# Order of the first loads, the gate block of the last stage, and the products of the linear attention

## The chip, the cores and the metric

The kernel runs on one core of a Trainium2 chip. The metric is the device time of one execution in microseconds; lower is better. TensorE does matrix products into PSUM (eight banks of 512 four-byte columns per partition), VectorE, ScalarE and GpSimd work on rows, SyncE issues most DMAs. Each engine runs its own instructions in the order in which they are written; semaphores tie the engines together.

## What is computed

A decoder of twelve layers (stages 0 to 11), each followed by a layer norm of the sum with its input, on 8 sequences of 100 tokens of 256 features, with a context of 361 tokens per sequence. All arithmetic is in four-byte floats. Two layers matter here. Stage 6 is a gated linear attention with 8 heads of 32 features:

```
q, k, v = (heads(Wq), heads(Wk), heads(Wv))     # of the rms-normed x; q, k rotated (rope)
beta, ig, og = (gate(Wbeta, bbeta), gate(Wig, big), gate(Wog, bog))
def step(M, inp):                               # over the tokens
    q_t, k_t, v_t, f_t, g_t, o_t = inp          # f = beta, g = ig, o = og
    M = M * f_t[..., None, None] + g_t[..., None, None] * scale * (k_t[..., :, None] * v_t[..., None, :])
    y_t = jnp.einsum('bhd,bhde->bhe', q_t, M) * o_t[..., None]
```

The kernel writes the recurrence out as a decayed mask per head (a scan over the tokens), which multiplies the scores of q and k before they multiply v. Stage 11 is a mixture of experts, of which this is the head and the end:

```
def _rmsnorm(x, g):
    return x * jax.lax.rsqrt(jnp.mean(x * x, axis=-1, keepdims=True) + eps) * g
scores = jax.nn.sigmoid(u @ centroids)
gpk, i_topk = jax.lax.top_k(scores, K)          # K = 2 of 8
gk = gpk / scores.sum(axis=-1, keepdims=True)
return u + h_s + h_r                            # and x + this, so x twice
```

## The kernel before

Everything is written by hand in blocks: a block holds one list of instructions per engine, and at its exit all engines meet. The order inside a list is the order of the code; no scheduler changes it. X holds the tokens (100 partitions, 8 batches, 256), XT their transpose (features on partitions), ps the eight PSUM banks. `program` runs the stages one after another; ahead of each stage SyncE issues the load of the next stage's weights (its "pack"), and the four computing engines wait for the stage's own pack.

**Start** (L3766 to L3774, in `program`). SyncE issues five loads: features (XT), pack 0, tables, tokens (X), context (ctxT). It waits for features, tables and tokens (a count of 48), then the block ends and stage 0 begins with projections of XT. The context has a semaphore of its own, waited for at stage 1. The tables hold the identity for transposes and the masks.

**Stage 6, `l2_attn`.** A hardware loop of two turns, each with four batches (TURN = 4, index j). In a turn TensorE transposes the normed tokens into hT; computes per batch v with the gates (L3120, one bank, 280 columns) and then q and k (L3125, the next bank, four parts of 128 features by 100 tokens); then the rotated q and k of all batches (L3133, with weights whose halves are swapped); then beta turned (L3139) and spread over the rows (L3144), the scores (L3151), the heads (L3157), the turned output (L3162) and the output product (L3167). VectorE copies v out of PSUM, makes the rotation in three instructions per batch (sine product L3204, cosine product L3206, sum L3208), scans the decayed mask (L3213, two per batch), weighs it with the scores (L3220, two per batch), and does the norm. ScalarE copies q and k and makes the gates' sigmoid. GpSimd makes the entries of the scan (L3099) and, after each rotation, a padded q (L3103): q repeated for the four heads that share a tile of 128 features, with the other heads' rows zeroed, so that a score product runs over all 128 rows.

**Stage 11, `l3_ffn`.** First block: logits on TensorE (L2479), sigmoid on ScalarE, the choice of two of eight and the gates on VectorE, the gates turned on TensorE (L2499) and stored by ScalarE (L2504); SyncE loads the first expert's weights. Second block: VectorE squares and sums the tokens (L2940), GpSimd makes the root per batch (L2915, L2917), VectorE scales (L2944) and doubles X (L2946) in turn, TensorE transposes each batch into its own bank (L2924), ScalarE copies it twice with two gains (L2933 into xs, L2934 into xr). Then `experts` runs 40 experts' units, and `experts_tail` the last norm.

## Time and profile before

| | us |
|---|---|
| median of 3 runs | 2661.86 |
| lowest, highest | 2661.77, 2664.53 |
| profiled execution, whole time | 2663.2 |
| profiled execution, span | 2661.4 |
| TensorE busy in the span | 2260.9 (85%) |
| VectorE busy | 1539.0 (58%) |
| ScalarE busy | 1147.5 (43%) |
| GpSimd busy | 466.6 (18%) |
| mean granted TensorE clock | 0.902 of 2.4 GHz |

The busy times are sums over stages with different limits. Stage 6 takes from about 1329 to 1450 us of the span, the head of stage 11 from 2263 to 2287. The profile's timeline gives each instruction's start and duration, and in square brackets how long its engine had stood idle and what ended that; "PEld" is TensorE's weight load.

### The profile page before, as it was taken

The numbers are of one execution on the slowest core, as the hardware profiler recorded it, in microseconds if no ns is written. First come the engines' busy times: TensorE is split into PE (matmuls) and PEld (weight loads), VectorE is DVE, ScalarE is ACT, GpSimd is POOL, SyncE is SP. The second block draws the span as 40 slices with busy tenths as digits, with TensorE's granted clock in tenths as the row PEclk, the third lists the DMA queues.
The fourth block names the chain that finished last, engine by engine and source line by source line (L and its number), as shares of the span: only waits on it lengthen the run. The fifth ranks groups of instructions, "written<-read, shape, count | busy, mean of one in ns | idle before, by whom it ended". The sixth has DMA issues, their size and how long they took to land. (4 is left out here: it accounts for less than half of the span.)

```text
span 2661.4 us, 42960 instructions
## 1 busy us (share of the span) xinstructions
PE 2260.9 (85%) x15050; PEld 1791.9 (67%) x15050; DVE 1539.0 (58%) x3604; ACT 1147.5 (43%) x3103; POOL 466.6 (18%) x681
## 2 busy tenths in 40 slices
PE   6799664659999976879878969799987999899997
PEld 4566432227777744569867648799975665799997
DVE  3566658996555653545555535456544555555555
ACT  4566344543434424533211634343321565455553
POOL 0200018982000010100143410000013222100001
PEclk8899788899999986669988979899977999799999
DMA  3000012210000013324200024232200000233331
GB/s 108 9 2 2 32 66 76 71 53 32 1 1 1 1 49 117 97 103 149 78 36 5 1 60 125 75 110 90 90 33 9 6 8 1 86 107 109 104 110 61
DMA packets 46180, 151.37 MB, mean 57 GB/s; under 512 B 16967, under 2 KB 19115, under 8 KB 43960
## 3 DMA queue, kind: packets, MB, share of 16 engines
q1 hardware_dynamic: 46012, 149.21, 17.6%
q8 instruction: 96, 1.57, 0.2%
q14 instruction: 72, 0.59, 0.1%
HBM read 137.70 MB, written 11.50 MB: 56 GB/s over the span
## 5 line engine op out<-in xcount | busy, mean ns | idle before, releaser
L2410 PE MATMUL ps<-l1a_zc,tables_sb 128*128 128x400 f32 x256 | 107.8, 553 | 96.3 <-POOL l1a_zc L2339 60.3
L2410 PEld LDWEIGHTS ps<-l1a_zc,tables_sb 128*128 128x128 f32 x256 | 46.9, 200 | 157.1 <-POOL l1a_zc L2339 88.5
L1912 ACT ACTIVATE l1x_probs<-ps,l1x_nmax 100x361 f32<-100x361 f32 x128 | 70.7, 558 | 164.5 <-DVE l1x_nmax L1987 164.5
L2350 POOL TENSOR_TENSOR l1a_dbx<-l1a_dx,l1a_rows 128x400 f32<-128x400 f32 x128 | 130.3, 1055 | 7.0 <-DMA l1a_rows<-l1a_rows_spilled 4.9
L2758 DVE TENSOR_TENSOR l3f_act_out<-l3f_act_out,l3f_gates 128x800 f32<-128x800 f32 x80 | 79.4, 993 | 81.8 <-ACT l3f_act_out L2714 81.8
L2762 DVE TENSOR_TENSOR l3f_hg_low<-l3f_act_out,l3f_hg_high 128x800 fp32r<-128x800 f32 x80 | 79.5, 993 | 62.9 <-ACT l3f_hg_high L2720 62.9
L2714 ACT ACTIVATE l3f_act_out<-ps,l3f_biases 128x800 f32<-128x800 f32 x80 | 74.3, 929 | 91.7 <-PE ps L2603 90.7
L2363 ACT ACTIVATE ps<-l1a_delta,weights 128x400 f32<-128x400 f32 x128 | 76.5, 598 | 81.2 <-DVE ps L2393 53.2
L2602 PE MATMUL ps<-l3f_x_high,l3f_w_high 128*128 128x400 f32 x320 | 111.4, 348 | 0.0
L2601 PE MATMUL ps<-l3f_x_high,l3f_w_low 128*128 128x400 f32 x320 | 110.7, 346 | 0.5 <-DVE l3f_w_low L2692 0.5
L2603 PE MATMUL ps<-l3f_x_low,l3f_w_high 128*128 128x400 f32 x320 | 110.6, 346 | 0.0
L2602 PE MATMUL ps<-l3f_hg_high,l3f_w_high 128*128 128x400 f32 x320 | 110.2, 344 | 0.0
L2601 PE MATMUL ps<-l3f_hg_high,l3f_w_low 128*128 128x400 f32 x320 | 110.0, 344 | 0.0
L2603 PE MATMUL ps<-l3f_hg_low,l3f_w_high 128*128 128x400 f32 x320 | 110.0, 344 | 0.0
L1026 ACT ACTIVATE l3x_probs<-l3x_s_sb,l3x_nmax 100x361 f32<-100x361 f32 x128 | 75.3, 589 | 68.3 <-DVE l3x_nmax L1115 64.3
L2720 ACT ACTIVATE l3f_hg_high<-l3f_act_out 128x800 fp32r<-128x800 f32 x80 | 69.9, 874 | 72.4 <-PE ps L2603 62.5
L1024 ACT ACTIVATE l0x_probs<-ps,l0x_nmax 100x361 f32<-100x361 f32 x128 | 70.7, 557 | 64.8 <-DVE l0x_nmax L1122 57.9
L2602 PE MATMUL ps<-l2f_x_high,l2f_w_high 128*128 128x400 f32 x272 | 95.0, 349 | 0.0
L2601 PE MATMUL ps<-l2f_x_high,l2f_w_low 128*128 128x400 f32 x272 | 94.3, 347 | 0.0
L2603 PE MATMUL ps<-l2f_x_low,l2f_w_high 128*128 128x400 f32 x272 | 94.2, 346 | 0.0
L2393 DVE TENSOR_TENSOR_SCAN ps<-ps,l1a_dbx 128x400 f32<-128x400 f32 x86 | 84.6, 994 | 16.7 <-POOL l1a_dbx L2350 9.8
L1115 DVE CUSTOM_DVE_ANT_0 l3x_s_sb<-ps,l3x_mask_b 100x361 f32<-100x361 f32 x128 | 63.2, 531 | 44.7 <-PE ps L931 44.4
(662 smaller groups left out, 6454.7 us busy)
## 6 DMA issues: line engine op xcount, KB each, us to landing
l3f_landing<-l_ffn_units SPq DMA_DIRECT2D x40, 513.0 KB, 3.6
l3f_gates<-l3f_gates SPq DMA_DIRECT2D x40, 400.0 KB, 3.4
l2x_a_taps<-l2x_taps_spread SPq DMA_DIRECT2D x8, 1912.5 KB
l2f_landing<-l_ffn_units SPq DMA_DIRECT2D x17, 771.0 KB, 4.5
l1a_rows<-l1a_rows_spilled SPq DMA_DIRECT2D x32, 400.0 KB, 3.4
l1f_gates<-l1f_gates SPq DMA_DIRECT2D x16, 800.0 KB, 4.1
l1f_positions<-l1f_staged SPq DMA_DIRECT2D x16, 621.9 KB
l1f_landing<-l_ffn_units SPq DMA_DIRECT2D x16, 512.0 KB, 3.2
```

The costliest lines, as they stand in the source:

```text
L1024: last = act.activation(probs[:, n % 2, r, 0:KEYS], score_bank(r), ACT.Exp, bias=nmax[:, n % 2, r:r + 1], accum_out=sums)
L1026: last = act.activation(probs[:, n % 2, r, 0:KEYS], s_sb[:, h % 3, r % 2, :], ACT.Exp, scale=-1.0, bias=nmax[:, n % 2, r:r + 1], accum_out ...
L2350: pool.tensor_tensor(dbx[:, n % BUFS, :], dx[:, j, m, :], rows[:, g % RING, 0, :], ALU.mult).then_inc(s.dbx_ready, 1)
L2363: act.activation(da(n), delta_h[:, m, j, :], ACT.Exp, scale=a_log[:, m, i:i + 1]).then_inc(s.da_ready, 1)
L2393: dve.tensor_tensor_scan(z(n), da(n), dbx[:, n % BUFS, :], 0.0, ALU.mult, ALU.add).then_inc(s.scan_done, 1)
L2410: pe.matmul(y_bank(m), st.ident, zc[:, n % DONE, :], start=(i == 0), stop=(i == NS - 1)).then_inc(s.sum_done, 1)
L2601: pe.matmul(out, r(w_lo), r(x_hi), start=start, stop=False)
L2602: pe.matmul(out, r(w_hi), r(x_hi), start=False, stop=False)
L2603: return pe.matmul(out, r(w_hi), r(x_lo), start=False, stop=stop)
L2714: act.activation(halves(act_out, t), st.ps[:, bank:bank + 2, 0:HALF], ACT.Gelu, bias=col(sl, 2 + t if geglu else t)).then_inc(s.gelu_done, 1)
L2758: dve.tensor_tensor(hg[:, t, :], act_out[:, t, :], gates[sl][:, 0, :], ALU.mult).then_inc(s.hg_gated, 1)
L2762: dve.tensor_tensor(hg_low[:, t, :].bitcast(F32R), hg[:, t, :], hg_high[:, t, :], ALU.subtract).then_inc(s.hg_ready, 1)
```

## The change

Three things are edited.

1. *Start.* Pack 0 is issued first, then features, tables and tokens. SyncE waits for features and tables alone (a count of 32). The tokens have a semaphore `x_loaded`, awaited by VectorE alone at the head of stage 0. The context is issued after the block, ahead of pack 1. One semaphore less is left for each of the two sets (69, not 70).
2. *Stage 11.* The two blocks become one. VectorE squares all batches, waits for one root instruction over eight columns, scales all batches, picks the gates, and doubles X at the end. TensorE makes the logits, the transposes (into half banks of banks 4 to 7, the second four after ScalarE has read the first), then turns the gates. ScalarE does the sigmoid, the 32 copies and the gates' store.
3. *Stage 6.* q and k are laid out as four parts (q's two tiles of 128 features, then k's) of all four batches of a turn, so each product has 400 columns; the plain ones stand behind all four v products, the rotated ones behind these. The three instructions of the rotation then work on a part, no more on a batch. The padded q and its table are gone: a score product runs over a head's own 32 rows, at the tile position of these rows, four such products side by side into four banks; scores and weighing go in pairs of batches, and the heads of a batch wait for its whole pair.

The diff, cut to its core:

```diff
@@ -2872,78 +2872,66 @@
...
-        with stage_sems(nc, GATE_SEMS + ["marks_set"]) as s, nc.Block(no_gpsimd_drain=True) as block:
...
-            with stage_sems(nc, ["sq_ready", "ms_ready", "rms_ready", "xn_ready", "xn_turned", "xs_done", "twice_done"]) as s, nc.Block(no_gpsimd_drain=True) as block:
+            turned = lambda j: st.ps[:, 4 + j % 4, j // 4 * KT * S:(j // 4 + 1) * KT * S].rearrange("p (k t) -> p k t", k=KT)
+            sems = ["sq_ready", "ms_ready", "rms_ready", "xn_ready", "xn_turned", "xs_done", "twice_done"]
+            with stage_sems(nc, GATE_SEMS + ["marks_set"] + sems) as s, nc.Block(no_gpsimd_drain=True) as block:
...
-                    for j in range(B):
...
-                        pool.tensor_tensor(rrms[:, j:j + 1], ms[:, j:j + 1], st.minus_half[0:S, :], ALU.pow).then_inc(s.rms_ready, 1)
+                    gate.pool_marks(pool, s)
+                    pool.wait_ge(s.sq_ready, B)
+                    pool.tensor_scalar(ms[:], ss[:], 1.0 / D, EPS, ALU.mult, ALU.add).then_inc(s.ms_ready, 1)
+                    pool.wait_ge(s.ms_ready, 1)
+                    pool.tensor_tensor(rrms[:], ms[:], st.minus_half[0:S, :].to_broadcast([S, B]), ALU.pow).then_inc(s.rms_ready, 1)
...
+                    gate.tensor_logits(pe, st, s, st.XT, st.w["f11gate"].rearrange("p (k e) -> p k e", k=KT))
...
+                        if j >= 4:
+                            pe.wait_ge(s.xs_done, 2 * KT * (j - 3))
                         for k in range(KT):
-                            last = pe.transpose(st.ps[:, j, k * S:(k + 1) * S], xn[:, j, k * P:(k + 1) * P], st.ident[0:S, 0:S])
+                            last = pe.transpose(turned(j)[:, k, :], xn[:, j, k * P:(k + 1) * P], st.ident[0:S, 0:S])
+                    gate.tensor_turn(pe, st, s)
...
+                    act.activation(gate.scores[:, :, 0:E], gate.logits(st), ACT.Sigmoid).then_inc(s.score_ready, 1)
...
-                            ps = st.ps[:, j, k * S:(k + 1) * S]
...
+                            act.activation(xs[:, k, j, :], turned(j)[:, k, :], ACT.Copy, scale=st.w["f11gs"][:, k:k + 1]).then_inc(s.xs_done, 1)
+                            act.activation(xr[:, k, j, :], turned(j)[:, k, :], ACT.Copy, scale=st.w["f11gr"][:, k:k + 1]).then_inc(s.xs_done, 1)
+                    gate.scalar_store(act, st, s)
...
                         dve.scalar_tensor_tensor(xn[:, j, :], x_b, 1.0, x_b, ALU.mult, ALU.mult, accum_out=ss[:, j:j + 1]).then_inc(s.sq_ready, 1)
+                    dve.wait_ge(s.rms_ready, 1)
...
-                        x_b = st.X[:, j, :]
-                        dve.wait_ge(s.rms_ready, j + 1)
-                        dve.tensor_scalar(xn[:, j, :], x_b, rrms[:, j:j + 1], None, ALU.mult).then_inc(s.xn_ready, 1)
-                        dve.wait_ge(s.xn_ready, j + 1)
-                        dve.tensor_tensor(x_b, x_b, x_b, ALU.add).then_inc(s.twice_done, 1)
+                        dve.tensor_scalar(xn[:, j, :], st.X[:, j, :], rrms[:, j:j + 1], None, ALU.mult).then_inc(s.xn_ready, 1)
+                    out, scores, left = gate.vector_pick(dve, s)
...
+                    dve.tensor_tensor(out, out, gate.wide(gate.rtotal), ALU.mult).then_inc(s.gate_ready, 1)
+                    dve.wait_ge(s.xn_ready, B)
+                    for j in range(B):
+                        dve.tensor_tensor(st.X[:, j, :], st.X[:, j, :], st.X[:, j, :], ALU.add).then_inc(s.twice_done, 1)
@@ -3067,8 +3055,7 @@
...
-        qk, rqk = sb("qk", [P, TURN, 2 * KT, S]), sb("rqk", [P, TURN, 2 * KT, S])
-        q_pad = sb("q_pad", [P, TURN, H, S])
+        qk, rqk = sb("qk", [P, 2 * KT, TURN, S]), sb("rqk", [P, 2 * KT, TURN, S])
@@ -3098,10 +3085,6 @@
...
-                    pool.wait_ge(s.rotated, j + 1)
-                    for m in range(KT):
-                        pool.tensor_tensor(q_pad[:, j, m * HPT:(m + 1) * HPT, :], wide(qk[:, j, m, :], HPT),
-                                           head_mask.unsqueeze(2).to_broadcast([P, HPT, S]), ALU.mult).then_inc(s.q_spread, 1)
@@ -3119,20 +3102,15 @@
...
+                for turned in range(2):
                     for i in range(2 * KT):
-                        w, m = (wq, wk)[i // KT], i % KT
+                        w, m = ((wq, wk), (wrq, wrk))[turned][i // KT], i % KT
+                        if turned:
+                            pe.wait_ge(s.vg_done, 2 * (i + 1))
                         for k in range(KT):
-                            last = pe.matmul(st.ps[:, 2 * j + 1, i * S:(i + 1) * S], w[:, k, m * P:(m + 1) * P], hT[:, j, k, :],
+                            last = pe.matmul(st.ps[:, 2 * i + 1 - turned, 0:TURN * S], w[:, k, m * P:(m + 1) * P], hT[:, :, k, :],
                                              start=(k == 0), stop=(k == KT - 1))
-                    last.then_inc(s.qk_ready, 1)
-                for j in js:
-                    pe.wait_ge(s.vg_done, 2 * (j + 1))
-                    for i in range(2 * KT):
-                        w, m = (wrq, wrk)[i // KT], i % KT
-                        for k in range(KT):
-                            last = pe.matmul(st.ps[:, 2 * j, i * S:(i + 1) * S], w[:, k, m * P:(m + 1) * P], hT[:, j, k, :],
-                                             start=(k == 0), stop=(k == KT - 1))
-                    last.then_inc(s.rqk_ready, 1)
+                        last.then_inc((s.qk_ready, s.rqk_ready)[turned], 1)
                 for j in js:
...
@@ -3144,15 +3122,19 @@
...
-                for j in js:
-                    pe.wait_ge(s.decay_ready, 2 * (j + 1))
-                    pe.wait_ge(s.q_spread, KT * (j + 1))
-                    for h in range(H):
-                        last = pe.matmul(st.ps[0:S, 2 * j + h // 4, (h % 4) * S:(h % 4 + 1) * S], qk[:, j, KT + h // HPT, :], q_pad[:, j, h, :],
-                                         start=True, stop=True)
+                pe.wait_ge(s.rotated, 2 * KT)
+                for first in range(0, TURN, 2):
+                    pe.wait_ge(s.decay_ready, 2 * (first + 2))
+                    for j in range(first, first + 2):
+                        for m in range(KT):
+                            at = (KT * (j - first) + m) * S
+                            for r in range(HPT):
+                                group = slice(HD * r, HD * (r + 1))
+                                last = pe.matmul(st.ps[0:S, 2 * first + r, at:at + S], qk[group, KT + m, j, :], qk[group, m, j, :], start=True, stop=True,
+                                                 tile_position=(HD * r, 0))
                     last.then_inc(s.scores_ready, 1)
                 for j in js:
-                    pe.wait_ge(s.weighed_ready, 2 * (j + 1))
+                    pe.wait_ge(s.weighed_ready, HPT * (j // 2 + 1))
...
@@ -3176,7 +3158,7 @@
...
-                    act.activation(qk[:, j], tiles(2 * j + 1, 2 * KT), ACT.Copy).then_inc(s.qk_done, 1)
+                    act.activation(qk[:, j], tiles(2 * j + 1, TURN), ACT.Copy).then_inc(s.qk_done, 1)
@@ -3201,9 +3183,9 @@
...
-                    dve.tensor_tensor(rqk[:, j], tiles(2 * j, 2 * KT), wide(sin, 2 * KT), ALU.mult).then_inc(s.rope_step, 1)
+                    dve.tensor_tensor(rqk[:, j], tiles(2 * j, TURN), wide(sin, TURN), ALU.mult).then_inc(s.rope_step, 1)
-                    dve.tensor_tensor(qk[:, j], qk[:, j], wide(cos, 2 * KT), ALU.mult).then_inc(s.rope_step, 1)
+                    dve.tensor_tensor(qk[:, j], qk[:, j], wide(cos, TURN), ALU.mult).then_inc(s.rope_step, 1)
@@ -3212,12 +3194,12 @@
...
-                for j in js:
-                    dve.wait_ge(s.decay_ready, 2 * (j + 1))
-                    dve.wait_ge(s.scores_ready, j + 1)
-                    for i in range(2):
-                        part = decay[:, j, 4 * i:4 * i + 4, :]
-                        dve.scalar_tensor_tensor(part, st.ps[0:S, 2 * j + i, 0:4 * S].rearrange("s (h t) -> s h t", h=4), float(HD) ** -0.5, part,
+                for first in range(0, TURN, 2):
+                    dve.wait_ge(s.decay_ready, 2 * (first + 2))
+                    dve.wait_ge(s.scores_ready, first // 2 + 1)
+                    for r in range(HPT):
+                        part = decay[:, first:first + 2].rearrange("s j (m r) t -> s j m r t", r=HPT)[:, :, :, r, :]
+                        dve.scalar_tensor_tensor(part, st.ps[0:S, 2 * first + r, 0:4 * S].rearrange("s (j m t) -> s j m t", j=2, m=KT), float(HD) ** -0.5, part,
                                                  ALU.mult, ALU.mult).then_inc(s.weighed_ready, 1)
@@ -3766,18 +3748,19 @@
...
+                sp.dma_start(packs[stages[0]], dram[f"pack{stages[0]}"]).then_inc(pack_loaded[stages[0]], 16)
                 sp.dma_start(st.XT[:], dram["x_features"]).then_inc(start_loaded, 16)
-                sp.dma_start(packs[stages[0]], dram[f"pack{stages[0]}"]).then_inc(pack_loaded[stages[0]], 16)
                 sp.dma_start(st.tables[:], dram["tables"]).then_inc(start_loaded, 16)
-                sp.dma_start(st.X[:], dram["x_tokens"]).then_inc(start_loaded, 16)
-                sp.dma_start(st.ctxT[:], dram["ctx_features"]).then_inc(ctx_loaded, 16)
-                sp.wait_ge(start_loaded, 48)
+                sp.dma_start(st.X[:], dram["x_tokens"]).then_inc(x_loaded, 16)
+                sp.wait_ge(start_loaded, 32)
...
         for n, i in enumerate(stages):
+            if n == 0:
+                nc.sync.dma_start(st.ctxT[:], dram["ctx_features"]).then_inc(ctx_loaded, 16)
...
+                if n == 0 and eng is nc.vector:
+                    eng.wait_ge(x_loaded, 16)
```

How the instructions stand in a row, before (-) and now (+), line numbers of each kernel. SyncE at the program's start (weights is pack 0 there, of 128x2048):

```order
-L3769 DMA XT<-x_features 128x1600
-L3770 DMA weights<-pack 128x2048
-L3771 DMA tables_sb<-tables 128x342
-L3772 DMA X<-x_tokens 100x2048
-L3773 DMA ctxT<-ctx_features 128x5776
-L3766 UNCONDITIONAL_BRANCH
+L3749 UNCONDITIONAL_BRANCH
+L3751 DMA weights<-pack 128x2048
+L3752 DMA XT<-x_features 128x1600
+L3753 DMA tables_sb<-tables 128x342
+L3754 DMA X<-x_tokens 100x2048
+L3748 UNCONDITIONAL_BRANCH
+L3763 DMA ctxT<-ctx_features 128x5776
```

The context moved behind the block's exit (the last branch), and the pack to the front.

TensorE in a turn of stage 6, before, from the second batch's products to the heads:

```order
L3120 MATMUL ps<-weights,l2a_hT 100x280 x2
L3125 MATMUL ps<-l2a_hT,weights 128x100 x8
L3133 MATMUL ps<-l2a_hT,weights 128x100 x32
L3139 MATMUL ps<-tables_sb,l2a_vg 8x100 x4
L3144 MATMUL ps<-l2a_beta_pad,tables_sb 100x100 x32
L3151 MATMUL ps<-l2a_q_pad,l2a_qk 100x100 x32
L3157 MATMUL ps<-l2a_vg,l2a_decay 100x32 x32
```

and now, the whole of it:

```order
L3103 MATMUL ps<-weights,l2a_hT 100x280 x8
L3111 MATMUL ps<-l2a_hT,weights 128x400 x16
L3117 MATMUL ps<-tables_sb,l2a_vg 8x100 x4
L3122 MATMUL ps<-l2a_beta_pad,tables_sb 100x100 x32
L3133 MATMUL ps<-l2a_qk 100x100 x32
L3139 MATMUL ps<-l2a_vg,l2a_decay 100x32 x32
```

The first two rows of before stand there four times in turn, once per batch; 64 products of 100 columns became 16 of 400.

VectorE at the head of stage 11 (MAX to MATCH_REPLACE pick the two experts, and stand in both):

```order
+L2921 SCALAR_TENSOR_TENSOR l3f_xn,l3f_ss<-X 100x256 x8
+L2924 TENSOR_SCALAR l3f_xn<-X,l3f_rrms 100x256 x8
 L2487 MAX l3f_top<-l3f_scores 100x8 x8
 L2489 COPY l3f_picked<-l3f_top 100x8x2
 L2492 MATCH_REPLACE l3f_left<-l3f_picked,l3f_scores 100x14 x8
-L2899 TENSOR_REDUCE l3f_total<-l3f_scores 100x8
-L2901 RECIPROCAL l3f_rtotal<-l3f_total 100x8
-L2902 TENSOR_TENSOR l3f_gate<-l3f_scores,l3f_left 100x8x8
-L2904 TENSOR_TENSOR l3f_gate<-l3f_gate,l3f_rtotal 100x8x8
-L2875 UNCONDITIONAL_BRANCH
-L2936 UNCONDITIONAL_BRANCH
-L2940 SCALAR_TENSOR_TENSOR l3f_xn,l3f_ss<-X 100x256 x8
```

Squares and scaling moved ahead of the choice, and the block's exit between gates and squares is gone.

## Rows read from the trace of the kernel before

**Rows 1.** Start: a wait and a landing, then timeline (start us, us, engine, line).
```profile
SPq L3766 <- DMA X<-x_tokens: 11.0, 1, 11.0
...
DMA to landing us min/median/max: 6.5/6.5/6.5
...
1.24 0.42 SPq L3770 DMA_DIRECT2D weights<-pack  x1
...
14.89 0.33 SPq L3783 DMA_DIRECT2D weights<-pack  x1
...
15.32 7.20 PE L1322 MATMUL ps<-XT,weights 128*128 128x400 f32 x16 [15.32 <-PEq L3766]
...
21.21 1.18 DVE L1575 TENSOR_SCALAR l0a_q_pad<-ps,tables_sb 128x400 f32<-128x400 f32 x2 [21.21 <-PE ps L1322]
```

**Rows 2.** Timeline, TensorE: 400-column records (stage 0), projections of stage 6.
```profile
24.79 2.95 PE L1322 MATMUL ps<-XT,weights 128*128 128x400 f32 x8
...
1335.99 2.07 PE L3120 MATMUL ps<-weights,l2a_hT 128*100 128x280 f32 x4
...
1340.38 1.11 PE L3120 MATMUL ps<-weights,l2a_hT 128*100 128x280 f32 x4
...
1341.33 1.92 PE L3125 MATMUL ps<-l2a_hT,weights 128*128 128x100 f32 x16
...
1348.50 7.31 PE L3133 MATMUL ps<-l2a_hT,weights 128*128 128x100 f32 x64
```

**Rows 3.** Timeline, first turn of stage 6: rotation and scans, and GpSimd's entries.
```profile
1350.49 0.57 DVE L3204 TENSOR_TENSOR l2a_rqk<-ps,weights 128x400 f32<-128x400 f32 x1 [3.03 <-PE ps L3133]
...
1352.28 0.57 DVE L3204 TENSOR_TENSOR l2a_rqk<-ps,weights 128x400 f32<-128x400 f32 x1
...
1354.19 1.85 POOL L3099 TENSOR_TENSOR l2a_entries<-tables_sb,l2a_vg 100x800 f32<-100x800 f32 x1
...
1355.07 2.22 DVE L3206 TENSOR_TENSOR l2a_qk<-l2a_qk,weights 128x400 f32<-128x400 f32 x1
...
1362.12 7.15 DVE L3213 TENSOR_TENSOR_SCAN l2a_decay<-ps,l2a_entries 100x400 f32<-100x400 f32 x8
```

**Rows 4.** Timeline: 32-row scores of stage 0; scores, weighing, heads of stage 6.
```profile
36.05 1.67 PE L1387 MATMUL ps<-l0a_kT,l0a_q_pad 32*100 32x100 f32 x32
...
1364.03 6.94 PE L3151 MATMUL ps<-l2a_q_pad,l2a_qk 128*100 128x100 f32 x64
1369.19 3.91 DVE L3220 SCALAR_TENSOR_TENSOR l2a_decay<-ps,l2a_decay 100x400 f32<-100x400 f32 x8
1370.81 5.76 PE L3157 MATMUL ps<-l2a_vg,l2a_decay 100*100 100x32 f32 x64
...
1431.13 7.30 PE L3157 MATMUL ps<-l2a_vg,l2a_decay 100*100 100x32 f32 x64
```

**Rows 5.** Windows: busy us (records) of PE, PEld, DVE, ACT, POOL; PEclk; DMA share, GB/s.
```profile
1436.00:1438.00 2.00, 2.00 (x14) 2.00 (x13) 0.22 (x1) 0.00 (x0) 0.00 (x0) 0.50 0.00 0
```

**Rows 6.** Head of stage 11, timeline and instructions by tile (ns min/median/max, first and last start).
```profile
2263.33 5.50 PE L2479 MATMUL ps<-weights,XT 128*100 128x8 f32 x32 [1.19 <-PEq L760]
...
L2064 POOL TENSOR_TENSOR l0f_rstd<-l0f_vareps,minus_half x1: 1674/1674/1674, 312.8 to 312.8; 100x8 f32<-100x8 f32 x1
...
2271.86 0.23 DVE L2904 TENSOR_TENSOR l3f_gate<-l3f_gate,l3f_rtotal 100x64 f32<-100x64 f32 x1
...
2273.68 0.83 ACT L2504 ACTIVATE l3f_gateT<-ps 10x800 f32<-10x800 f32 x1 [4.59 <-PE ps L2499]
...
L2940 DVE SCALAR_TENSOR_TENSOR l3f_xn<-X x8: 418/418/424, 2274.9 to 2277.3; 100x256 f32<-100x256 f32 x8
...
L2944 DVE TENSOR_SCALAR l3f_xn<-X,l3f_rrms x8: 345/348/353, 2277.6 to 2282.9; 100x256 f32<-100x256 f32 x8
...
L2933 ACT ACTIVATE l3f_xs<-ps,weights x16: 342/444/560, 2278.7 to 2285.5; 128x100 f32<-128x100 f32 x16
...
2286.63 0.20 ACT L2682 ACTIVATE l3f_biases<-l3f_landing 128x2 f32<-128x2 f32 x1 [0.34 <-PEq L2910]
```

## What the change will do to the time

> **What bounds the kernel now.** The change touches three places, so I read only the stretches that hold them, each in order of time: the waits and issues of the first 25 us, one turn of the linear attention (stage 6, two turns of four batches), and the gate work at the head of the last stage. The page's averages say little here, since no engine is the limit throughout.
>
> At the start nothing computes: SyncE waits 11.0 us for the tokens X, the block ends, the next DMA is issued at 14.89 and TensorE starts at 15.32, while the first pack had landed at 1.24 + 6.5 = 7.7 [rows 1].
>
> In a turn of the linear attention the limit passes from TensorE (projections, 1336 to 1350) to VectorE (rotation, scans, weighing, 1350.5 to 1373) and back to TensorE (heads and output) [rows 2 to 4].
>
> In the last stage the gate block and the normalising block run one behind the other: logits from 2263.33, gates ready at 2271.86 + 0.23, squares only from 2274.9, and the experts begin at 2286.63 [rows 6]. Almost every engine there is idle half the time, because a block's exit separates work that doesn't depend on each other.
>
> **The first loads.** X and the context leave the wait; they are not removed. Left in front of the exit are pack, features and tables: 1024, 800 and 171 KB (from the shapes). Pack and features, 1824 KB, took until 7.7, some 280 KB/us, so the tables' 171 KB add 0.6: about 8.3. X ended the wait some 0.4 before 14.89 (what a block's exit costs), at 14.5. Upper bound of the gain: 14.5 - 8.3 = 6.2. Lower bound: if the 2795 KB up to X arrive evenly, 1995 KB are there at 10.3 to 10.6, a gain of 3.8. I take **5.5**, near the upper end, because the landing of the pack is a measured row, and take off a little for the delay between landing and release, of which no row shows the size. The swap of features and pack costs nothing: both are awaited. The context's issue moves behind SyncE's wait and ahead of the next pack; both are needed at stage 1 only. X is now awaited by VectorE at the stage's head; behind that wait stands all its work. Its first instruction stood at 21.21 [rows 1], so 15.7 after the gain, and X, without the context beside it, should land by 11 to 14. Cost nothing; without that cover, as much as X is late.
>
> **Linear attention, one turn.** A four-byte matmul leaves two records.
> - Projections. Before, one batch took 1341.33 - 1340.38 = 0.95 for v and gates, and three batches take 1348.50 - 1340.38 = 8.12, 2.71 each, so q and k cost 1.76 a batch, 7.0 for four. Now each of the four 128-column parts of q and k covers all batches in two matmuls of 400 columns. Such a record costs a third of a us (eight in 2.95, tail included) [rows 2], so four parts cost 16 x 0.333 = 5.3. Saved: 1.7. All four v matmuls now stand first, still at the low clock; both orders pay for that, and I count no difference.
> - Rotation. The four rotations took from 1350.49 to the first scan at 1362.12, 11.6 us, though an undisturbed one takes 1352.28 - 1350.49 = 1.8. The excess stands beside GpSimd: the cosine product needs 2.22 when the entries (1.85) or the padded q run there [rows 3]. The padded q is gone; the entries are now all released early, at q and k's copies, and I find the last one ending 3 us behind the start of the rotated projections, so it meets one rotation. 4 x 1.8 + 1.1 = 8.3, and the first rotation starts 0.5 sooner (2 matmuls of 400 columns against 8 of 100). Saved: 3.3 + 0.5, with 1.7 from above 5.5; laid out step by step I get 5.9, and take **5.7**. Bounds: 4.0, if every rotation meets GpSimd once more, and 6.9 if none does.
> - Scores and weighing. The scans stay (8 in 7.15) [rows 3]. Scores cost 6.94 for 64 records before; the nearest row for 32-row ones is 1.67 for 32 at the low clock [rows 4]. The first pair's lie under the scans, the second pair's under the first pair's weighing (four of the eight in 3.91). But heads of batch 0 now wait for four weighings instead of two: before they started at 1370.81, 1.5 behind the last scan (1362.12 + 7.15); now 2.1. Cost: **0.5**.
> - The clock. In the second turn TensorE fell to the granted 0.50, 1.2 GHz, in the middle of the heads, where 14 records took 2.00 us, 0.143 each [rows 5]; 64 records took 7.30 there, against 5.76 in the first turn, nearly all at 2.4 GHz [rows 4]. Both turns entered the heads without a hole. Now TensorE has some 1 us of scores, 2.4 of nothing, 1 us of scores and 1 of nothing ahead of them. I expect the low clock from the heads' first matmul on: 64 x 0.143 = 9.2, so +3.4 in the first turn and +1.9 in the second. Bounds: 0 and 8 for both together.
>
> Two turns: 2 x (5.7 - 0.5) = 10.4, less 5.3: **5.1**.
>
> The Trainium skill speaks against this part in "TensorE: Matmul & The Clock Gate", section "Part 1: The HAM clock gate (the "warmup" mystery)": the array's clock is halved after a spell with little work and given back after sustained work. By that rule the holes cost what I count above; if it didn't bite, the sum would be 5.3 larger. "SBUF — State Buffer", section "SBUF: two separate sides", says that VectorE and GpSimd share a port pair as an exclusive lock. By a full lock the one rotation beside the last entries costs 1.85 instead of 1.1, 1.5 less gain over two turns.
>
> **Gate block.** One block instead of two. VectorE's eight squares need 2277.6 - 2274.9 = 2.7, from 2263.3 to 2266.1, beside the logits (5.50). GpSimd then makes eight roots at once: 1.67 by the row of the same shape, plus an estimated 0.3 for the scaling: 2268.1. The scaled tokens start at 2268.5; the logits end at 2268.83, so the new order costs TensorE nothing. ScalarE's 32 copies are the longest piece: the xs copies run from 2278.7 to 2285.5, 15 steps, so 0.45 a pair and 7.3 for all. From 2269.6 to 2276.9, then the gates' store (0.83): 2277.8. VectorE: scaling to 2271, pick and gates 3.3 at most (2268.83 to 2272.09), gates at 2274.2, turned by 2275.7, hidden under the copies; doubling X, 8 x 0.35, ends at 2277, hidden as well. With 0.4 for the exit the experts start at 2278.2 instead of 2286.63 [rows 6]: **8.4** less. Bounds: 6 if VectorE's chain slips by what the doubling cost between scalings, 10 if copies start at once after the squares. Awaited transposes (from the fifth batch on) find their half bank free: TensorE is four batches ahead of ScalarE. The first expert's weights were asked for at the block's start and land long before.
>
> **Sum.** 5.5 + 5.1 + 8.4 = 19.0. The profiled execution took 2663.2 (span 2661.4), so 2644.2; it is 1.3 over the median, 2661.86, against which I predict **2643**.
>
> **Rivals.**
> - The clock holds through the heads (turns as they were, or better): for it, the stretch before the heads is short; against it, the fall in both turns before. 2661.9 - 24.3 = 2637.5.
> - The start gains less: the tables arrive with X, 3.8 or less. For it, the transfers share the engines. 2644.7, and with a late X for VectorE 2646 to 2648.
> - The merged block doesn't overlap: the copies wait on VectorE's chain and the gates' store goes behind everything. 3 to 5 of the 8.4 lost: 2646 to 2648.
> - Slower than before: the low clock doesn't end with the heads but holds through most of both turns, since 400-column work and packed scores leave more holes. A us at the full clock costs 9.2/5.76 = 1.6 at the low one. To lose 19.0 and 5.3 more it must take 24.3/0.6 = 41 us of now fast work; in two turns there are about 65. 2668. Against it: projections of 400 columns keep TensorE busy without a pause for 13 us.
> - That the wait isn't shortened at all: X is issued behind the tables on the same queue, and its landing no longer counts for SyncE, so I give it nothing of its own.
>
> **Chances.** Forecast 0.50, clock holds 0.20, start smaller 0.14, gate smaller 0.13, slower 0.01, and 0.02 for a gain lost almost whole. A measurement of this kernel tells about 0.2%, 5.3 us, from no change. Faster by more 0.96, within 0.03, slower 0.01. The range takes in the clock's rival and both smaller gains: 2636 to 2649.
>
> **What the changed profile would show.** SyncE's wait ends on the tables' or features' landing and TensorE starts near 9.8; VectorE's first work isn't released by X. In a turn, rotations 1.8 apart with at most one long cosine product, scans from 5.7 earlier, a granted clock of 0.50 throughout the heads, 64 records in 9.2. In the last stage, 14.9 us between first logits and experts instead of 23.3, with ScalarE's copies unbroken. I would be wrong if X's wait or the tables came last after 11, if the heads took under 7, if a cosine product over 2 us appeared more than once a turn, or if the copies showed idle time ahead of them.

## The result, and the profile after

The changed kernel took 2635.07 us, the median of 4 executions (2632.63 to 2639.53), against 2662.81 for the kernel before in the same session (4 executions, 2661.77 to 2664.53). The ratio is 0.9897, 95% interval 0.988 to 0.9914: 27.7 us less, where 19.0 were forecast, and 2635.07 lies outside the range of 2636 to 2649. The profiled execution took 2632.63 (span 2630.9). Of all executions of the kernel before, one in a later session (2790.71 us, at a mean granted clock of 0.788) was in the chip's slow state and is left out throughout.

Read one by one, the three edited places did nearly what the working says. First the start: the waits of SyncE, then the timeline (start us, us, engine, line), kernel after.

```profile
SPq L3748 <- DMA tables_sb<-tables: 5.9, 1, 5.9
...
9.23 0.34 SPq L3763 DMA_DIRECT2D ctxT<-ctx_features  x1
...
9.66 8.61 PE L1322 MATMUL ps<-XT,weights 128*128 128x400 f32 x16 [9.66 <-PEq L3748]
...
16.96 1.18 DVE L1575 TENSOR_SCALAR l0a_q_pad<-ps,tables_sb 128x400 f32<-128x400 f32 x2 [16.96 <-PE ps L1322]
```

SyncE waits 5.9 us, for the tables, instead of 11.0 for X; TensorE starts at 9.66 instead of 15.32 [rows 1], 5.7 earlier (forecast 5.5). VectorE's first instruction is released by TensorE's products and not by X, so the wait that the change adds is covered.

Timeline of the two turns of stage 6, kernel after, and two windows of TensorE in the first turn's heads (busy us and records of PE, PEld, DVE, ACT, POOL; PEclk; DMA share, GB/s):

```profile
1335.14 10.91 PE L3111 MATMUL ps<-l2a_hT,weights 128*128 128x400 f32 x32
...
1342.06 0.57 DVE L3186 TENSOR_TENSOR l2a_rqk<-ps,weights 128x400 f32<-128x400 f32 x1 [6.20 <-PE ps L3111]
1342.55 1.23 DVE L3188 TENSOR_TENSOR l2a_qk<-l2a_qk,weights 128x400 f32<-128x400 f32 x1
...
1344.79 0.56 DVE L3188 TENSOR_TENSOR l2a_qk<-l2a_qk,weights 128x400 f32<-128x400 f32 x1
...
1349.03 7.15 DVE L3195 TENSOR_TENSOR_SCAN l2a_decay<-ps,l2a_entries 100x400 f32<-100x400 f32 x8
1352.80 0.96 PE L3133 MATMUL ps<-l2a_qk 32*100 32x100 f32 x32 [0.43 <-DVE l2a_decay L3195]
1356.10 3.92 DVE L3202 SCALAR_TENSOR_TENSOR l2a_decay<-ps,l2a_decay 100x400 f32<-100x400 f32 x8
1356.23 0.96 PE L3133 MATMUL ps<-l2a_qk 32*100 32x100 f32 x32 [2.47 <-DVE l2a_decay L3195]
1358.14 10.88 PE L3139 MATMUL ps<-l2a_vg,l2a_decay 100*100 100x32 f32 x64 [0.94 <-DVE l2a_decay L3202]
...
1416.53 10.88 PE L3139 MATMUL ps<-l2a_vg,l2a_decay 100*100 100x32 f32 x64 [0.66 <-DVE l2a_decay L3202]
```
```profile
1358.00:1360.00 2.00, 1.86 (x11) 1.86 (x12) 2.00 (x5) 0.00 (x0) 0.00 (x0) 0.50 0.00 0
1360.00:1362.00 2.00, 2.00 (x14) 2.00 (x14) 0.44 (x2) 0.00 (x0) 0.00 (x0) 0.50 0.00 0
```

One cosine product meets GpSimd (1.23), the others take 0.56, where before one took 2.22 [rows 3]. The four rotations with their sums last 1349.03 - 1342.06 = 7.0 instead of 11.6. From the turn's first h (1326.2, before 1332.6) to the scans it is now 22.8 instead of 29.5: 6.7 earlier a turn, forecast 5.7. The scores leave TensorE a hole of 2.47 and one of 0.94, and the granted clock is 0.50, 1.2 GHz, from the heads' first matmul on: 64 records take 10.88 in both turns, not 9.2. All four profiles with the edit of stage 6 and no products added to it show 10.87 or 10.88 in both turns; three profiles of the kernel before show 5.76 in one turn and 7.30 to 8.10 in the other, in one of them with the slow turn first.

The head of stage 11: timeline and, for the fourth row, instructions of a tile, kernel after.

```profile
2240.87 5.50 PE L2479 MATMUL ps<-weights,XT 128*100 128x8 f32 x32 [1.02 <-PEq L760]
...
2244.04 1.65 POOL L2891 TENSOR_TENSOR l3f_rrms<-l3f_ms,minus_half 100x8 f32<-100x8 f32 x1
2245.72 2.19 DVE L2924 TENSOR_SCALAR l3f_xn<-X,l3f_rrms 100x256 f32<-100x256 f32 x8 [2.06 <-POOL l3f_rrms L2891]
...
L2913 ACT ACTIVATE l3f_xs<-ps,weights x16: 344/456/582, 2246.8 to 2253.7; 128x100 f32<-128x100 f32 x16
...
2254.11 0.81 ACT L2504 ACTIVATE l3f_gateT<-ps 10x800 f32<-10x800 f32 x1
...
2255.26 0.20 ACT L2682 ACTIVATE l3f_biases<-l3f_landing 128x2 f32<-128x2 f32 x1 [0.34 <-PEq L2880]
```

From logits to experts it is 14.4 us instead of 23.3 [rows 6], 8.9 less; from the first instruction on the scores, as in the table further on, 8.7 less. ScalarE's copies run unbroken from 2246.8 to 2254.1, 7.3 as forecast, and they set the end.

The three places together: 5.7 + 4.5 (stage 6 as a whole, 6.4 earlier at its start and 10.9 at its end) + 8.7 = **18.9**, against a forecast of 19.0. The profile nevertheless is 30.5 us shorter than that of before. The other 11.6 lie in stages whose code is the same in both kernels: 2.4 and 4.2 in the two halves of stage 7, 7.0 in stage 9 and 0.7 in stages 0 to 5, of which stage 10 and the experts take 2.6 back. That is what the experiments are about.

### The profile page after: what moved, and what is told of

It is laid out like the page before. It is cut to its first block and busy times, and to the rows that moved or that the text cites. A ratio compares the mean times of both kernels' runs of the same rounds, so it can differ in the third digit from the quotient of the medians.

```text
span 2630.9 us, 42525 instructions
## 1 busy us (share of the span) xinstructions
PE 2242.1 (85%) x14858; PEld 1767.0 (67%) x14858; DVE 1529.6 (58%) x3604; ACT 1148.3 (44%) x3103; POOL 444.8 (17%) x651
## 3 DMA queue, kind: packets, MB, share of 16 engines
q1 hardware_dynamic: 46012, 149.21, 17.6%
## 5 line engine op out<-in xcount | busy, mean ns | idle before, releaser
L2602 PE MATMUL ps<-l3f_hg_high,l3f_w_high 128*128 128x400 f32 x320 | 110.2, 344 | 0.0
L2601 PE MATMUL ps<-l3f_hg_high,l3f_w_low 128*128 128x400 f32 x320 | 110.1, 344 | 0.0
```

The source lines that it names most:

```text
L2601: pe.matmul(out, r(w_lo), r(x_hi), start=start, stop=False)
L2602: pe.matmul(out, r(w_hi), r(x_hi), start=False, stop=False)
```

## The experiments

Two theories went in. **A**: the edits are worth 19 to 20 us, and the rest is how long TensorE happens to be granted 1.2 GHz in untouched stages. **B**: an edit shortens a later stage for good, through layout, loads or semaphores.

**Each edit alone.** Three kernels, each the kernel before with one of the three edits.

```
e1_loads:  the start's loads of the change alone (wait for 32 instead of 48; x_loaded; context behind the block)
e2_attn:   l2_attn and the table list (no a6heads) of the change alone
e3_gate:   l3_ffn's merged gate block of the change alone
```

> The kernel before with the edit of the first loads alone. Both theories put TensorE's start near 9.7 instead of 15.3 and stage 0 some 5.7 us ahead. Theory A (the time not accounted for, some 9 us, lies in where the granted clock falls and rises in stages that the change doesn't touch, and moves with any shift in time): the whole comes out anywhere from 2 to 12 us below before, and stages 7 and 9 keep or lose low-clock time without an edit to them. Theory B (one of the three edits shortens a later stage directly, by its memory layout, its loads or its semaphores): this run gives 5.7 us and stages 7 and 9 last as before within 0.5 us, unless it is this edit.

> The kernel before with the edit of stage 6 alone (table of head rows gone too). Stage 6 itself: 4.5 us shorter, with the heads at the low clock in both turns. Theory A: the whole 0 to 12 us below before, the difference to 4.5 being low-clock time in stages 7 and 9. Theory B, if this is the edit that does it: stage 7 about 6 us and stage 9 about 7 us shorter as well, 17 us in all; if not, 4.5.

> The kernel before with the merged gate block of stage 11 alone. It stands behind stages 7 and 9, which can't feel it. Both theories: head of stage 11 8.5 us shorter, everything ahead of it as before. The experts behind it may gain or lose 1 us of clock. 2654.

Measured, in one session with 28 executions of before (median 2659.1 us): e1 2656.24 (12 executions, 2636.93 to 2659.41; ratio 0.9981, 0.996 to 1.0001), e2 2650.81 (0.9974, 0.996 to 0.9989), e3 2651.17 (0.996, 0.9942 to 0.9979). By the medians -2.9, -8.3 and -7.9: together -19.1. By the ratios it is -5.1, -6.9 and -10.6, together -22.6, and each of them can be off by 4 to 5.5 us; so the sum of the three fits 19 to 20 and doesn't exclude 27.7. What each execution shows is wide: e1 took 2637 to 2640 in three executions and 2652 to 2659 in nine, at mean clocks of 0.911 to 0.912 and 0.900 to 0.905. And e3, whose edit stands behind stage 9, has a stage 9 that is 6.9 shorter than in the profile of before. Code that comes later can't do that by layout of what runs before it; against B, and for A. In their own places the edits did as expected: start at 12.4 instead of 18.4, stage 6 4.7 shorter, head of stage 11 9.1 shorter (table below).

**Filling the holes ahead of the heads.** The changed kernel with products that nobody reads, behind the scores of each pair:

```diff
+                    for _ in range(3 if first else 9):
+                        last = pe.matmul(st.ps[0:S, 2 * first, 4 * S:5 * S], st.ident[:, 0:S], hT[:, 0, 0, :], start=True, stop=True)
                     last.then_inc(s.scores_ready, 1)
```

> The changed kernel with 9 products of 100 columns behind the first pair's scores and 3 behind the second pair's, into columns of PSUM that nobody reads; they add nothing to the result. They fill TensorE's holes between scans and heads. If these holes are why the heads run at 1.2 GHz, the clock now holds into the heads: 64 records in 5.8 to 7.3 us instead of 10.9, stage 6 some 7 us shorter over two turns; the whole then 2628 if the later stages keep their clock. If the heads' own few columns are why, the fall comes as before and stage 6 is as long or 0.5 us longer.

Timeline of TensorE in the two turns, f1_fill:

```profile
1354.60 1.83 PE L3136 MATMUL ps<-l2a_hT,tables_sb 128*100 128x100 f32 x18
1357.14 0.96 PE L3133 MATMUL ps<-l2a_qk 32*100 32x100 f32 x32 [0.71 <-DVE l2a_decay L3197]
1358.03 0.77 PE L3136 MATMUL ps<-l2a_hT,tables_sb 128*100 128x100 f32 x6
1359.05 8.89 PE L3141 MATMUL ps<-l2a_vg,l2a_decay 100*100 100x32 f32 x64 [0.24 <-DVE l2a_decay L3204]
...
1416.30 8.21 PE L3141 MATMUL ps<-l2a_vg,l2a_decay 100*100 100x32 f32 x64 [0.24 <-DVE l2a_decay L3204]
```

Two windows of the first turn's heads there, in the columns of the windows above:

```profile
1359.00:1361.00 2.00, 1.95 (x22) 1.95 (x23) 2.00 (x5) 0.00 (x0) 0.00 (x0) 1.00 0.00 0
1363.00:1365.00 2.00, 2.00 (x14) 2.00 (x13) 0.07 (x1) 0.00 (x0) 0.00 (x0) 0.50 0.00 0
```

The hole of 2.47 is 0.71, and the heads take 8.89 and 8.21 instead of 10.88 twice: they start at 2.4 GHz, and the clock falls in their course, though TensorE has no pause there. So the holes explain the fall ahead of the heads and not the one within them, which the second turn of before shows too [rows 5]. Stage 6 is 8.4 shorter than before instead of 4.5, so the holes that the packed scores leave cost about 4 us. That is less than expected: the heads were to take 5.8 to 7.3, stage 6 to be 7 shorter, the whole to be 2628. Median 2633.53 (6 executions; ratio 0.9904, 0.9881 to 0.9927).

**The same two programs again.** The decisive test needs no edit: before and after unchanged, profiled and timed anew.

> The changed kernel once more, unaltered, beside more executions of the kernel before. If the edits themselves are worth 19 to 20 us, as their single measurements sum to, and the other 8 us were the clock's place in the executions first compared, the median lies 17 to 22 us below the kernel before of the same batch (ratio 0.992 to 0.9935). If the whole change is worth 28 us, because one edit shortens a later stage for good, the ratio is again 0.990 or less.

> The kernel before, unaltered, profiled a second time. If the length of stage 9 varies between executions of one program (theory A), from its first probabilities to stage 10's it takes anything from 52 to 63 us, where the first profile shows 62.6; likeliest some 55, as in five kernels that differ from it elsewhere. If the edits shorten it for good (theory B), it takes 62 to 63 us again.

> The kernel before, profiled a third time; as for the second: under theory A one of the two lies at least 4 us from the first profile's 62.6 in stage 9, and stages that no edit touches (0, 7, 9, 10) explain the difference of the two spans within 1 us. Under theory B all stages repeat within 1 us.

> The changed kernel, unaltered, profiled a third time and timed again. Theory A, the edits are worth 19 to 20 us and the rest is the clock in untouched stages: the touched places repeat within 1 us (start 12.7, turn pair 119.4, gate head 14.4), stages 0, 7, 9, 10 scatter by several us, median 2636 to 2641, ratio 0.991 to 0.9935. Theory B: they repeat too, ratio 0.990 or less.

The softmax's turned probabilities of stage 9 (instructions by tile, ns min/median/max, first and last start) in three executions of the kernel before: the first profile, p1_before, p2_before.

```profile
L506 PE MATMUL ps<-tables_sb,l3a_probs x8: 374/374/374, 1991.8 to 2025.0; 100*100 100x100 f32 x8
```
```profile
L506 PE MATMUL ps<-tables_sb,l3a_probs x8: 247/251/374, 1988.4 to 2011.2; 100*100 100x100 f32 x8
```
```profile
L506 PE MATMUL ps<-tables_sb,l3a_probs x8: 374/374/374, 1988.8 to 2022.0; 100*100 100x100 f32 x8
```

The same instructions of the same program last from first to last 33.2, 22.8 and 33.2 us. Windows of this stretch, the first profile of before and then p1_before, which runs 3.4 us ahead:

```profile
1984.00:1994.00 10.00, 8.57 (x39) 7.58 (x38) 1.73 (x7) 3.82 (x11) 1.20 (x3) 0.50 0.14 60
1994.00:2004.00 10.00, 8.87 (x38) 7.82 (x39) 2.50 (x11) 2.18 (x8) 1.20 (x3) 0.50 0.01 2
2004.00:2014.00 10.00, 9.20 (x30) 6.58 (x30) 3.43 (x13) 1.95 (x7) 1.19 (x3) 0.50 0.00 0
2014.00:2024.00 10.00, 8.28 (x29) 6.25 (x30) 3.82 (x15) 1.48 (x5) 2.44 (x6) 0.50 0.00 0
```
```profile
1980.00:1990.00 10.00, 8.72 (x41) 7.97 (x41) 1.73 (x7) 3.71 (x10) 1.21 (x3) 0.50 0.19 82
1990.00:2000.00 10.00, 8.44 (x48) 6.91 (x46) 3.47 (x14) 2.89 (x11) 1.21 (x3) 0.77 0.01 2
2000.00:2010.00 10.00, 7.21 (x46) 5.74 (x47) 6.29 (x24) 2.39 (x9) 3.35 (x9) 1.00 0.00 0
```

Both enter at 0.50 and with nearly the same busy time (8.57 and 8.72 in the first ten us). In one the clock is back in the course of the second window, in the other TensorE works 87% of forty us at 1.2 GHz. Lengths of stages in us, each worked out from the first starts of two tiles (stage 0 from kT to stage 1's probabilities, 6 from h to stage 7's eh, 7 from eh to the keys behind it, which is its first half, 9 from its probabilities to stage 10's, 10 from there to the gates' scores, the head of 11 from scores to the experts' biases):

| kernel | start of kT | 0 | 6 | 7 | 9 | 10 | head of 11 | end |
|---|---|---|---|---|---|---|---|---|
| before | 18.4 | 100.3 | 123.9 | 112.5 | 62.6 | 221.1 | 23.1 | 2658.6 |
| p1_before | 17.8 | 99.5 | 123.8 | 110.7 | 52.2 | 221.2 | 23.2 | 2645.6 |
| p2_before | 18.1 | 97.0 | 123.8 | 112.9 | 62.6 | 222.5 | 23.1 | 2657.6 |
| e1_loads | 12.4 | 97.4 | 123.7 | 110.8 | 52.3 | 221.0 | 23.0 | 2632.6 |
| e2_attn | 18.0 | 101.8 | 119.2 | 110.0 | 54.3 | 225.8 | 23.3 | 2650.6 |
| e3_gate | 17.6 | 99.7 | 123.9 | 112.8 | 55.7 | 223.2 | 14.0 | 2646.5 |
| after | 12.7 | 99.8 | 119.4 | 110.1 | 55.6 | 222.9 | 14.4 | 2628.1 |
| a1_again | 12.7 | 97.1 | 119.5 | 110.1 | 54.2 | 225.8 | 14.4 | 2631.3 |
| p3_after | 12.2 | 102.2 | 119.5 | 110.1 | 54.3 | 225.8 | 14.4 | 2635.9 |
| f1_fill | 12.6 | 99.5 | 115.5 | 110.3 | 56.0 | 223.0 | 14.4 | 2628.9 |
| b3_burst | 18.6 | 99.5 | 123.8 | 112.8 | 48.5 | 222.9 | 23.0 | 2647.1 |
| s3_burst | 12.9 | 103.6 | 115.5 | 110.2 | 48.6 | 222.6 | 14.5 | 2627.5 |
| s6_burst | 12.4 | 97.0 | 115.5 | 110.2 | 51.7 | 225.8 | 14.4 | 2627.3 |
| g3_gatefill | 12.4 | 101.8 | 115.4 | 110.1 | 58.7 | 225.8 | 15.0 | 2634.8 |

Not in the table are stages 1 to 5 (1210.8 to 1219.0 in these profiles), the second half of stage 7 (146.0 to 150.2), stage 8 (260.3 to 261.3) and the experts (359.9 to 362.1).

The edited places repeat within 0.7 us in every profile that has the same edit. Stage 0 takes 97.0 to 103.6, stage 9 (without added products) 52.2 to 62.6, whatever the kernel. p1_before ends 13.0 before the first profile of the same program, 10.4 of it in stage 9. So the length of stage 9 is no work of the edits: there A holds and B falls. Times: a1 2637.5 (6 executions; before 2660.15; ratio 0.9923, 0.9896 to 0.9949), p3 2640.17 (6; before 2657.66; 0.9927, 0.9914 to 0.9939). All sessions together: before 2659.3, the median of 60 executions (2644.8 to 2668.4); after 2637.8, of 16 (2632.6 to 2641.1). The change is worth about **21.5**, not 27.7; the three sessions with both kernels give 27.7, 22.7 and 17.5. The forecast 19.0, a ratio of 0.9929, lies within the intervals of the two later ones.

The column of stage 7 is 110.0 to 110.3 in all eight profiles with the edit of stage 6, and 110.7 to 112.9, mean 112.1, in the six without. Windows of stage 7's first us, the first profile of before and then e2_attn, and one of s3_burst (below):

```profile
1452.00:1456.00 4.00, 2.40 (x5) 1.51 (x5) 1.97 (x7) 0.00 (x0) 0.00 (x0) 0.50 0.28 82
1456.00:1460.00 4.00, 4.00 (x9) 2.24 (x8) 0.51 (x1) 1.12 (x2) 0.00 (x0) 0.63 0.00 0
1460.00:1468.00 8.00, 6.78 (x27) 4.38 (x25) 3.33 (x5) 3.37 (x6) 4.24 (x5) 1.00 0.00 0
1468.00:1474.00 6.00, 4.84 (x14) 3.49 (x15) 1.66 (x1) 0.98 (x2) 2.65 (x4) 0.72 0.00 0
```
```profile
1450.00:1454.00 4.00, 2.65 (x5) 1.60 (x6) 1.64 (x7) 0.00 (x0) 0.00 (x0) 0.50 0.23 71
1454.00:1458.00 4.00, 4.00 (x14) 2.52 (x13) 0.91 (x1) 1.70 (x4) 0.82 (x1) 0.95 0.00 0
1458.00:1466.00 8.00, 5.61 (x24) 3.71 (x23) 2.93 (x4) 2.80 (x5) 4.78 (x6) 1.00 0.00 0
1466.00:1472.00 6.00, 6.00 (x29) 4.17 (x28) 2.12 (x2) 4.05 (x7) 1.27 (x2) 1.00 0.00 0
```
```profile
1463.00:1469.00 6.00, 6.00 (x14) 4.11 (x15) 1.66 (x1) 1.90 (x3) 1.53 (x2) 0.50 0.00 0
```

In e2_attn the clock is back some 2.3 us sooner and doesn't fall a second time (0.72 before, 1.00 with the edit). The same holds for after, a1_again, p3_after and f1_fill: 25 us into the stage these five are 2.5 to 3.1 ahead of the six without the edit. This gain behind the edit, by the way stage 6 ends, hadn't been in the sum. But it isn't the whole column. In s3_burst, s6_burst and g3_gatefill, whose code up to here is that of f1_fill, the clock does fall a second time and the 2.5 us are lost again; they, p1_before and e1_loads make up 2.0 to 2.7 us in the last 25 us of the column. And the column of stage 10 goes the other way: 222.6 to 225.8, mean 224.7, in the eight with the edit, 221.0 to 223.2, mean 222.0, in the six without. Taken together, the stages behind the edit show no net gain that stands out of the scatter.

**Idle products ahead of stage 9.** Three products of 400 columns in the block in which TensorE waits for GpSimd to clear buffers, in the kernel before (b3) and in f1_fill (s3), six in f1_fill (s6).

```diff
+            @block.tensor
+            def _(pe):
+                if name == "l3a":
+                    for _ in range(3):
+                        pe.matmul(st.ps[0:S, 0, 0:4 * S], st.ident[:, 0:S], xT[:, 0, 0:4, :], start=True, stop=True)
```

> The kernel before, with three idle products of 400 columns on TensorE added in the block that clears the buffers of stage 9 (layer 3's self-attention), where TensorE waits for GpSimd anyway; their results are read by nobody. Theory A (the 9 us not explained by the edits lie in how long the low clock holds in untouched stages, stage 9 above all): the products take 4 us at 1.2 GHz, of which at most 0.5 us prolongs the block; stage 9's low clock lasts at most 34 us instead of 58.0, the profiled stage takes at most 40 us instead of 45.2 from its first to its last probabilities, and the median is 3 to 10 us below the kernel before. Theory B (the stage's length follows from the edits' layout and loads and not from the clock): stage 9 stays at 45 us and the median within 0.1% of before, or 0.5 us above it.

> The changed kernel with the idle products ahead of the heads of stage 6 (as in f1_fill) and the same three products of 400 columns ahead of stage 9. Theory A: stage 9's low clock lasts at most 34 us, in most executions, as in the profiles of the changed kernel already; so little to gain in the median over f1_fill (0 to 4 us), but the slower executions disappear. Theory B: 0.5 us slower than f1_fill.

> The same with six products instead of three: 8 us at 1.2 GHz, so some 4.5 us of them stand in the way. Theory A: if three products are too few to bring back 2.4 GHz before the projections of stage 9 and six are enough, the stage's low clock ends by the first projections (16 us of them at 1.2 GHz, 8 at 2.4 GHz) and the kernel is 5 to 10 us faster than with three. Theory B: 4.5 us slower than f1_fill, and stage 9 otherwise as it was.

Instructions of stage 9's turned probabilities again, first b3_burst, then g3_gatefill (below), which has the same three products in front:

```profile
L512 PE MATMUL ps<-tables_sb,l3a_probs x8: 247/251/252, 1990.9 to 2011.1; 100*100 100x100 f32 x8
```
```profile
L512 PE MATMUL ps<-tables_sb,l3a_probs x8: 248/313/374, 1979.1 to 2005.7; 100*100 100x100 f32 x8
```

Windows of TensorE in b3_burst, from the added products on:

```profile
1980.00:1984.00 4.00, 3.77 (x6) 1.57 (x6) 0.00 (x0) 0.00 (x0) 2.09 (x2) 0.50 0.81 258
1984.00:1988.00 4.00, 3.16 (x21) 2.33 (x20) 0.52 (x2) 1.82 (x3) 0.80 (x2) 0.87 0.43 181
```

In b3's profile all eight run at 2.4 GHz, the clock is back 5 us into the stage, and stage 9 takes 48.5 instead of 62.6 or 52.2: the stage is shorter with more work in it, and the difference lies in the clock. But in time no gain is shown: the median of b3, 2656.61, is 3.5 below that of before in its session, while the ratio is 1.0003 (0.9981 to 1.0024; 12 executions, 2643.45 to 2669.11). And in g3's profile half of the eight are at 1.2 GHz in spite of the same three products. Three products bring the clock back in some executions only; here A was right on the mechanism and wrong on its reliability. s3: 2632.08 (2623.28 to 2639.96; ratio 0.9896, 0.9866 to 0.9927), its longest execution is only 1.1 below the changed kernel's longest of that session, 2641.01, so the slower executions did not disappear. s6: 2632.03, not 5 to 10 below s3, but also not 4.5 above it, with six executions within 2628.43 to 2632.66 (ratio 0.99, 0.9874 to 0.9926). Neither theory's number came: no gain and no loss over three products is shown. Both are 5.4 to 5.5 below the changed kernel of the same session (2637.5), of which the filled holes of stage 6 are 4; that the products ahead of stage 9 add to it isn't shown.

**Idle products in the gate block.** s3 with two more products of 400 columns behind the turned gates:

```diff
                     gate.tensor_turn(pe, st, s)
+                    for _ in range(2):
+                        pe.matmul(st.ps[0:S, 1, 0:4 * S], st.ident[:, 0:S], st.XT[:, 0, 0:4, :], start=True, stop=True)
```

> The changed kernel with all idle products together: those ahead of the heads of stage 6, the three of 400 columns ahead of stage 9, and two more of 400 columns behind the turning of the gates in the last stage, where TensorE waits 2.54 us for the block to end. Their results are read by nobody. If the holes in the gate block keep the clock low, it rises before or in the bias products (5.67 us for eight at 1.2 GHz), which then take 3 to 4 us, and the experts' stage is 2 to 4 us shorter than in s3_burst: median 2628 to 2631. If the clock stays low until the experts have run for as long as now, nothing changes: 2632.

Timeline, the experts' bias products, in s3_burst and then in g3_gatefill:

```profile
2254.80 5.67 PE L2640 MATMUL ps<-l3f_gateT,weights 10*128 10x400 f32 x8 [2.54 <-PEq L2886]
```
```profile
2264.21 3.08 PE L2640 MATMUL ps<-l3f_gateT,weights 10*128 10x400 f32 x8 [0.42 <-PEq L2886]
```

They run at 2.4 GHz, as expected. The experts' stage is 2.1 shorter (359.9 instead of 362.0) and the head 0.5 longer. In the time it can't be seen: 2638.17 (6 executions, 2631.04 to 2645.72; ratio 0.992, 0.9902 to 0.9939), not the expected 2628 to 2631, and 2.0 below the changed kernel of the same session; its profile has stages 0 and 9 at 101.8 and 58.7. Inconclusive: a gain of 1.6 is smaller than what stage 9 alone varies by.

## Why the prediction was wrong

- **The step that failed is the base of the sum, with the time of all stages without an edit taken as fixed.** "The profiled execution took 2663.2 (span 2661.4), so 2644.2; it is 1.3 over the median, 2661.86." The sum takes the three places off these numbers and so puts the change of every other stage at nothing, without a reason. The runs showed in its place: in the two profiles first compared 11.6 us less in stages without an edit, 7.0 of it in stage 9, whose length is 62.6, 52.2 and 62.6 in three profiles of one program. The base itself came from one short session, whose spread of 3 us looked like the kernel's. The kernel's own spread is 2644.8 to 2668.4 and its median 2659.3; the first four of it lay 3.5 above, and the first four of after (2635.07) 2.7 below theirs (2637.8). These 6.2 are most of the 8.7 us between 19.0 and 27.7. 2659.3 - 19.0 would have been 2640.3, 2.5 above what 16 executions show.
- **The range had no term for it.** Its bounds came from the edited places alone. The trace of before shows the granted 0.50 through at least forty us of stage 9 (windows above), though TensorE is 87% busy there. At 2.4 GHz that stretch is up to 10 us shorter, as p1_before shows, and should have widened a range of 13.
- **The other 2.5** stay open. By the means of three profiles of each kernel the edited places are worth 18.7 (5.6, 4.4 and 8.7) and the rest 3.5: stage 9 gives 4.4, the two halves of stage 7 1.9 and 1.2, while stage 10 takes 3.2 back and the others 0.8. Three profiles each can't tell such a rest from chance. Open is also whether the changed kernel ever has the long stage 9 (62.6): none of its three profiles has, two of three of before have.
- **Start**: forecast 5.5, measured 5.7. The wait ends on the tables, as said. TensorE's first 16 records take 8.61 instead of 7.20 [rows 1], which was not in the sum. It is no work of the edit: the first records start 0.67 apart and the later ones 0.34, and e1_loads, with the same edit, takes 7.5 for the 16. Stage 0 as a whole takes 97.0 to 103.6.
- **Projections and rotation**: 5.7 a turn, measured 6.7, within the bounds of 4.0 to 6.9 and near the case that no rotation meets GpSimd: the one that does costs 0.7, not 1.1. Its cosine product starts at 1342.55, 0.8 before GpSimd's entries end (1343.35), so it waits about that rest and no more.
- **Weighing in pairs**: forecast 0.5 from the first scan to the heads, measured (1358.14 - 1349.03) - (1370.81 - 1362.12) = 0.4.
- **The heads' clock**: the mechanism is right and the term was mis-sized. 64 x 0.143 = 9.2 divided a window's 2.00 us by its 14 records [rows 5], but a window also counts the records that its edges cut: the one of after shown above has 14 in 2.00 us as well, while a turn's 64 take 10.88, 0.170 each. The extra over before is 5.1 and 3.6 instead of 3.4 and 1.9, 0.7 over the upper bound of 8 for both. With 2 x (6.7 - 0.4) - 8.7 = 3.9 stage 6 comes out near its measured 4.5 (forecast 5.1); the 0.6 between are open.
- **Gate block**: forecast 8.4, measured 8.9 from the logits on, as the forecast counts. Copies 7.3 as worked out; they start 6.0 behind the first logits, not 6.3.
- **Rivals.** "The clock holds", 2637.5, is next to the measured time and yet wrong: the clock didn't hold. Had only the total been read, it would have passed for confirmed. The merged block overlapped, and the low clock did end with the output of each turn.

The rule of the Trainium skill on TensorE's clock ("TensorE: Matmul & The Clock Gate", section "Part 1: The HAM clock gate (the "warmup" mystery)"), a fall after a spell with little work and a return after sustained work, agrees with the fall behind the hole of 2.47. The return doesn't come out by it: the heads keep TensorE busy for 10.9 us at 0.50, and stage 9 does so for 83 to 92% of forty us. There the measurement decides. What no row of the first profile could show is that in such a stretch the return differs from execution to execution.

## What to carry to other kernels

Price the edited places from rows, but take the base from many executions, and look in the profile for long stretches at the low clock with a busy TensorE: each is a term of the range, in us, though no edit touches it. Judge a forecast by its places, stage by stage against several profiles of both kernels, before its total is believed. An edit can also change in which state TensorE enters the next stage; here that gave 2.5 to 3.1 us at the start of stage 7 in five of eight profiles, and the whole time doesn't show it. Short idle products in a hole ahead of a long run of narrow matmuls gave 4 us of stage 6.

## What the hardware showed that was not expected

- One program takes 2644.8 to 2668.4 us, and a stage without any edit 52.2 or 62.6: TensorE at 8.3 to 9.2 of 10 us busy stays at 1.2 GHz for 40 us in one execution and is back at 2.4 in the second of four such windows in the other.
- A turn's 32 products of 32 columns for the heads (64 records) keep TensorE busy without a pause for 10.9 us and the granted clock stays 0.50 throughout. With the hole ahead of them filled they start at 2.4 GHz, and the clock falls in their course.
- Three extra products of 400 columns ahead of a stage can make it 4 to 14 us shorter (48.5 and 48.6 against 52.2 to 62.6), or leave it at 58.7.
